# Three small moves in a two-layer attention kernel: row normalisation to GpSimd, an earlier pair of products, and masks written by ScalarE

## What is computed

```python
x = x + L0_xattn(layernorm(x), ctx, ctx)          # 16 heads, no mask
x = x + L0_ffn(layernorm(x))
x = x + L1_xattn(layernorm(x), ctx, ctx, mask)    # logits + mask * -1e9
x = x + L1_moe(layernorm(x))

def act_quant(x):                                 # in L0_ffn, for each row
    scale = 127.0 / clip(max(abs(x)), 1e-05)
    return clip(round(x * scale), -128, 127) / scale
```

## Time and profile before

| | |
|---|---|
| median of 3 runs | 509.7 us (509.5 to 510.54) |
| the profiled execution | 508.18 us |
| its span, first to last instruction | 506.4 us |
| PE busy | 443.3 us (88%) |
| PEld busy | 363.2 us (72%) |
| DVE busy | 345.9 us (68%) |
| ACT busy | 301.6 us (60%) |
| POOL busy | 226.5 us (45%) |
| mean granted clock of TensorE | 0.981 |

### The profile page before, as it was taken

One profiled execution on the slowest core, in us unless ns is written; L12 is line 12 of the kernel. 1 busy time (PEld: TensorE's weight loads), 2 busy tenths in 40 slices (PEclk: granted clock), 3 DMA queues, 4 the chain that ended last, 5 costly groups with the idle time before them and its releaser, 6 DMA issues.

```text
span 506.4 us, 11481 instructions
## 1 busy us (share of the span) xinstructions
PE 443.3 (88%) x3709; PEld 363.2 (72%) x3709; DVE 345.9 (68%) x1233; ACT 301.6 (60%) x649; POOL 226.5 (45%) x455
## 2 busy tenths in 40 slices
PE   3689999999998779967999999999999889899960
PEld 2477777777775668856778878777777579899960
DVE  6767787878783267877887788787878266444424
ACT  5237776767767448874466756566556555455630
POOL 4752464123216245767200225354453566666650
PEclk9999999999999989989999999999999999999995
DMA  6463323332405995034253234333320301332107
GB/s 216 150 223 105 115 85 116 102 101 77 137 4 207 426 415 213 2 105 130 84 159 113 88 107 158 118 122 94 112 61 2 87 23 39 85 85 82 53 15 249
DMA packets 40698, 61.55 MB, mean 122 GB/s; under 512 B 6121, under 2 KB 30506, under 8 KB 39232
## 3 DMA queue, kind: packets, MB, share of 16 engines
q1 hardware_dynamic: 38080, 56.20, 34.0%
q0 software_dynamic: 2272, 4.24, 2.6%
q10 hardware_dynamic: 288, 0.39, 0.3%
HBM read 31.45 MB, written 29.23 MB: 120 GB/s over the span
## 4 chain that ended last, share of the span: by engine, by line
PE 45%; DVE 10%; issue 5%; ACT 4%; DMA 3%; SPq 2%; POOL 1%; POOLq 0%; DVEq 0%; ACTq 0%
PE ps L1698 6%; PE ps L1658 6%; PE ps L1740 6%; PE ps L1743 5%; PE ps L1889 5%; PE ps L1900 5%; ACT probs L1023 2%; PE ps L1867 1%; DMA k_blocks<-y_dram 1%; DVE ps L1303 1%; PE ps L1954 1%; PE ps L1674 1%; SPq L544 1%; PE ps L1675 1%; PE ps L1676 1%
## 5 line engine op out<-in xcount | busy, mean ns | idle before, releaser
L1023 ACT ACTIVATE probs<-ps 128x512 f32<-128x512 f32 x256 | 147.0, 598 | 79.6 <-PE ps L1743 75.0
L1658 PE MATMUL ps<-k_blocks,q_stacks 128*128 128x256 f32 x512 | 117.9, 314 | 6.4 <-DVE row_max L1289 3.0
L1289 DVE TENSOR_REDUCE row_max<-ps 128x2 f32<-128x512 f32 x144 | 94.9, 686 | 26.9 <-PE ps L1658 25.7
L1743 PE MATMUL ps<-q_stacks,k_blocks 128*128 128x256 f32 x512 | 104.9, 288 | 1.2 <-DMA q_stacks<-maxT 1.0
L1303 DVE CUSTOM_DVE_ANT_0 ps<-ps,mask_q 128x256 f32<-128x256 f32 x224 | 89.8, 452 | 20.6 <-PE ps L1658 18.9
L1743 PEld LDWEIGHTS ps<-q_stacks,k_blocks 128*128 128x128 f32 x512 | 86.8, 189 | 20.8 <-issue 10.6
L1658 PEld LDWEIGHTS ps<-k_blocks,q_stacks 128*128 128x128 f32 x512 | 82.6, 197 | 13.9 <-issue 4.3
L1698 PE MATMUL ps<-probs,v_aug 128*32 128x256 f32 x1024 | 68.5, 385 | 4.3 <-ACT probs L1023 3.1
L817 POOL TENSOR_SCALAR max_split<-row_max 128x16 fp32r<-128x16 f32 x32 | 6.5, 204 | 124.3 <-issue 93.0
L1740 PE MATMUL ps<-mask_k,neg_mask_eye 128*128 128x512 f32 x128 | 54.5, 426 | 0.0
L739 POOL DMA_INDIRECT y_dram<-x_ring x39 | 39.1, 1003 | 22.6 <-ACT x_ring L1102 14.2
(11 more groups left out here) (217 smaller groups left out, 760.1 us busy)
## 6 DMA issues: line engine op xcount, KB each, us to landing
slots_dram<-x_ring SPq DMA_DIRECT2D x1, 10400.0 KB, 30.1
q_stacks<-q_dram SPq DMA_DIRECT2D x32, 256.0 KB
k_blocks<-k_dram SPq DMA_DIRECT2D x128, 48.0 KB
q_dram<-qk_parts SPq DMA_DIRECT2D x16, 256.0 KB, 2.9
k_dram<-qk_parts SPq DMA_DIRECT2D x16, 256.0 KB, 2.9
mask_in<-host_mask SPq DMA_DIRECT2D x8, 512.0 KB, 3.6
experts<-host_experts SPq DMA_DIRECT2D x1, 4096.0 KB, 39.1
x_ring<-slots_dram SPq DMA_DIRECT2D x39, 65.0 KB
```

What stands on the lines that cost most here:

```text
L1023: eng.activation(probs[:, n // HPS % 2, n % HPS, :, :].rearrange("p k q -> p (k q)"), ps[:, head_bank(BANKS_T, n)[0], :], ACT.Exp).then_in ...
L1289: eng.tensor_reduce(row_max[:, :, n], ps[:, head_bank(BANKS_S, n)[0], :].rearrange("p (i k) -> p i k", i=NT), AX.X, ALU.max).then_inc(a.s_ ...
L1658: mm = eng.matmul(ps[:, bank, i * S:(i + 1) * S], q_stack[r][:, st, i * P:(i + 1) * P], k_blocks[r][:, st, j, :], start=not masked, stop=n ...
L1743: mm = eng.matmul(ps[:, bank, k * S:(k + 1) * S], k_blocks[r][:, st, j, k * P:(k + 1) * P], q_stack[r][:, st, :], start=(l == 0), stop=(l ...
```

## The change

Three edits.

1. **Layer 0's `ln_apply`** goes from VectorE (n = 11) to GpSimd, right behind `ln_power`. `quant_factors` stays on VectorE at n = 13 and waits for it.
2. **Layer 0, step 1 of each body on TensorE**: `shifted` of head 1 and then the transposes of half 1's maxima stand ahead of `weighted_v`. Before, the transposes stood at step 0 and `shifted` of head 1 behind `weighted_v`. ScalarE's `out_copy` of half 1 moves from n = 0 to n = 1.
3. **Layer 1**: for the heads 5, 7, 8, 11, 13 and 15 the mask matmul is gone. ScalarE writes `-320000 * mask_k` into the bank (`mask_seed`) at steps 2, 4, 5, 8, 10 and 12, behind the exponential that frees it, and the two products add to what stands there.

```diff
-    "max1": (0, 2),
+    "max1": (None, 2),
-    "a_out1": (0, 0),
+    "a_out1": (1, 0),
-    "d_ln": (11, 12),
+    "d_ln": (None, 12),
...
+        SEEDED = (5, 7, 8, 11, 13, 15)
+        SEED_STEPS = (2, 4, 5, 8, 10, 12)
...
                 if exists(b - 1):
                     ln_power(eng, s, b - 1)
+                    if l == 0:
+                        ln_apply(eng, s, b - 1)
...
+                    if l == 1 and exists(b) and n in SEED_STEPS:
+                        mask_seed(b, SEEDED[SEED_STEPS.index(n)])
...
+            def mask_seed(b, n):
+
+                if n == SEEDED[0]:
+                    eng.wait_ge(a.k_k, b + 1)
+                eng.wait_ge(a.p_sb, b * 16 + n - 2 if n < H - 1 else b * 16 + 12)
+                eng.activation(ps[:, head_bank(BANKS_T, n)[0], :],
+                               mask_k[b % 3][:, :, :].bitcast(F32).rearrange("p i k -> p (i k)"),
+                               ACT.Copy, scale=-MASK_A).then_inc(a.t_seed, 1)
...
                     if exists(b + 1):
                         scores(eng, l, b + 1, 1 - r, n)
+                    ahead = l == 0 and n == at["pv"] % HPS and exists(b)
+                    if ahead:
+                        shifted(b, r, n)
+                        second_max(b)
                     if n % HPS == at["pv"] % HPS:
...
-                    if exists(b):
+                    if exists(b) and not ahead:
                         shifted(b, r, n)
...
-                if l == 1:
+                seeded = l == 1 and n in SEEDED
+                if seeded:
+                    eng.wait_ge(a.t_seed, b * len(SEEDED) + SEEDED.index(n) + 1)
+                elif l == 1:
                     eng.matmul(ps[:, bank, :], neg_mask_eye[:, :], mask_k[b % 3][:, :, :].rearrange("p i k -> p (i k)"),
                                start=True, stop=False)
```

More of the change, by code:

```diff
@@ L320, in __init__ @@
                     return
+                self.t_seed = s("t_seed")
                 self.k_in, self.k_q, self.k_k = s("mask_in"), s("mask_q"), s("mask_k")
@@ L1340, in body @@
                         residual_stats(eng, l, b - 1)
[L1341 to L1345, removed]
+                    if l == 1 and n == at["d_ln"] and exists(b - 1):
+                        ln_rows(eng, b - 1, 1 - r)
                     if l == 0 and n == at["d_quant"] and exists(b - 1):
@@ L1721, in body, with second_max @@
                             weighted_v(eng, l, b, r, (n - at["pv"]) // HPS)
-                    if exists(b):
+                    if exists(b) and not ahead:
                         shifted(b, r, n)
                     extras(b, r, n)
+            def second_max(b):
+                if after(b, 0):
+                    eng.wait_ge(a.o_sb, b * 2 - 1)
+                max_transposes(eng, l, b, 1)
             def shifted(b, r, n):
@@ L1743, in shifted @@
                     mm = eng.matmul(ps[:, bank, k * S:(k + 1) * S], k_blocks[r][:, st, j, k * P:(k + 1) * P],
-                                    q_stack[r][:, st, :], start=(l == 0), stop=(l == 0 or k == NT - 1))
+                                    q_stack[r][:, st, :], start=(l == 0), stop=(l == 0 or k == NT - 1),
+                                    skip_group_check=seeded)
                 mm.then_inc(a.t_ps, 1)
@@ L1762, in extras @@
                 if n == at["max1"] and exists(b):
-                    if after(b, 0):
-                        eng.wait_ge(a.o_sb, b * 2 - 1)
-                    max_transposes(eng, l, b, 1)
+                    second_max(b)
                 if n == at["qk"] and two_ahead(l, b):
```

## The result

The changed kernel took **507.74 us** in the median of 20 runs (505.31 to 511.17), the kernel before 509.72 in 20 runs between them (508.29 to 513.47): 0.9956 of its time, 95% interval 0.9939 to 0.9973, so 2.0 us faster by the medians (1.4 to 3.1 by the interval) where 4.9 were forecast. The direction is right and the time lies in the range; the size is off by more than half. They are not always the quotient of the two medians shown, and differences in us are worked out from the ratios where nothing else is said.

The account below looks back on a forecast made before the run. The prediction took TensorE to set the pace in both layers, with two waits in each layer 0 body. Its terms, +1.0 - 2.7 - 5.0 + 1.8 = -4.9 us, took 509.7 to 504.8 us, range 500.0 to 510.0.

Parts of the forecast that it names:

- Edit 1: Layer 0's normalised rows moved from VectorE to POOL: forecast +1.0 us in all.
- Steady bodies: Layer 0's steady bodies with rows on POOL: quantising factors start at the same time, a tie, 0 us.
- End of layer 0: Nothing covers the last two rows there: 1.60 us on POOL instead of 0.60 on VectorE, +1.0 us.
- The third rival, POOL late: Layer 0: rows on POOL take longer beside VectorE, delaying eight bodies; 517.6 us at twice the time; chance 0.06.
- Edit 2: Layer 0: head 1's products fill TensorE's hole before the transposes, 0.47 us in a steady body, -2.7 us together.
- Edit 3: Layer 1's six seeds: 0.71 us a body over seven bodies, -5.0 us, before the last body's cost.
- Heads 13 and 15: Layer 1: TensorE dense there with VectorE ahead, so both masks count, 2 x 0.24 = 0.47 us a body.
- The zeros for heads 5, 8 and 11: Layer 1: these masks lie inside or beside waits for other engines, so removing them gains 0.
- the 0.24 for head 7: Layer 1: this head's mask lies behind the wait for VectorE, so removing it gains 0.24 us a body.
- The rival in which VectorE binds all of layer 1: Layer 1: scores go at VectorE's pace with two banks, so seeds give nothing; 509.8 us; chance 0.11.
- Body 7: Layer 1's last body: seeds lengthen ScalarE's path, about 0.5 us plus 2 x 0.65 before the tanh, +1.8 us.
- The sum: Whole kernel: +1.0 - 2.7 - 5.0 + 1.8 = -4.9 us, forecast 504.8 us.

Follow-up runs that it names:

- the order alone: Kernel before with only head 1's two products and half 1's transposes moved in layer 0, rows on VectorE, no seeds: 508.16 us, ratio 0.9952.
- the two better kernels above: Kernel before with layer 0's new order, seeds for heads 7 and 13 except last body; rows on VectorE (0.9861), or on POOL for seven batches (0.9858).
- the seventh run: Changed kernel with one more 128x128 row on VectorE in each body of layer 1, behind head 12's maximum: 509.31 us in one run, bodies 20.41 us.

## Why the prediction came out as it did

**Edit 1, right.** Steady bodies 0 forecast, and 0 measured: 0.27 us less over layer 0's bodies, but that is a standstill of VectorE of 0.36 us, which goes from a body of layer 0 to one of layer 1 (last section). End of layer 0 +1.0 forecast, +1.06 measured (4.00 to 5.06). The third rival, POOL late, fell: a row took 806 ns beside VectorE's maxima. The rule of the Trainium skill behind it ("Perfetto Trace Analysis", Optimizing Scalar/DVE Operations) shows no effect in this trace.

**Edit 2, right.** -2.7 forecast. The transposes of body 1 and body 7 were 103.73 us apart and are 101.12, -2.6; by the projections -2.2, of which the order alone gives -2.0, and its own kernel is 2.5 us faster by the runs. A steady body gave 0.42 us and not 0.47. The transposes' wait went in the steady bodies, head 0's stayed.

**Edit 3, the step that failed.** "Heads 13 and 15: dense, with VectorE ahead. 2 x 0.24 = 0.47." One of the two counts. VectorE was ahead, idle for 0.55 us before head 14's maximum, and I took that for room. But it was idle because it waited for these very scores; the trip scores, maximum, scores through two banks took 1.60 us of TensorE's 1.65. The term should have been 2 x 0.24 = 0.48 a body, head 7 and head 13, and not 0.71: 7 x 0.48 = -3.4 in place of -5.0. The steady bodies show the 0.48. That the whole stretch to the seventh projection is 3.4 us shorter as well is in part luck. It also holds 0.5 for body 7's seeds and the 0.36 of VectorE's standstill, so the seeds brought some 4.3 us there; in the two better kernels above, which have neither, it is 3.8 and 3.9 us shorter. The surplus over 3.4 lies in the first and last bodies, where traces of one kernel also differ by up to 0.6 us. The zeros for heads 5, 8 and 11 and the 0.24 for head 7 stand in the steady bodies. Two masks give 0.48 (20.88 to 20.40), so a mask is worth 0.24, not the 0.13 of the Trainium skill's sustained spacing ("TensorE: Matmul & The Clock Gate", Back-to-back issue gap). The rival in which VectorE binds all of layer 1 named the right engine and the two banks, but let them eat all of the gain, by VectorE's amount of work, and that the seventh run excludes. (A small slip in the same part: from the first issue at 150.68 to the product at 153.05 it is 2.37 us, not 2.35. No `shifted` waited for a DMA in layer 1.)

**Body 7, right.** +1.8 forecast as 0.5 + 2 x 0.65; measured 0.5 + 1.2. What these seeds cost through the clock behind them, the prediction left out; by the traces it may be 1 us more.

**The sum.** With two masks in place of three the forecast would have been +1.0 - 2.7 - 3.4 + 1.8 = -3.3 us, where -4.9 stood. The four stretches measured give the same, -2.2 + 1.06 - 3.4 + 1.2 = -3.3 (body 7's 0.5 is in the -3.4). The runs gave -2.0 and -4.1 on two chips. The rest is the clock, which falls in some stretches outside the steady bodies, and in one execution of a kernel not in the same ones as in the next. In 56 runs of the kernel before on the chips of the experiments, the 24 with a mean clock of 0.973 to 0.977 took 510.0 us in the mean, the 7 at 0.967 or less 512.2. Of the changed kernel's 28, the 12 of the first class took 506.2, the 10 of the second 509.4: -3.8 and -2.8 at like clocks (in the second class 0.965 and 0.962 in the mean, so the changed kernel's were a little slower). That the change has no part in how often the clock falls isn't shown: two comparisons disagree on it (0.968 and 0.972), and the window behind body 7 speaks for a part.

## What to carry to other kernels

An engine that is idle before its step of a ping-pong isn't ahead: add up the whole round trip (product, reduction, next product in the same bank) and set it beside the other engine's work in between, since only that difference can be gained. Then offload the few instructions that count: two seeds of six gave the whole gain of a steady body, and the other four cost 0.5 us (heads 5, 8 and 11) and 0.6 us (head 15) in the last body, where nothing covered them. And leave the last pass of a loop as it was when an offload there has no partner to hide behind: the seeds of heads 13 and 15 cost 0.6 us each there, and the two rows on POOL 1.06 together, the whole difference between the two engines.

## What I had not expected of the hardware

- In one body of layer 1, always the same, VectorE stood still between two instructions with nothing to wait for, 0.25 us in this timeline of the changed kernel:

```profile
330.66 0.47 DVE L1279 RECIPROCAL rden<-ps 128x16 f32<-128x16 f32 x2 [0.52 <-PE ps L1877]
331.38 0.61 DVE L1285 TENSOR_TENSOR o_norm<-ps,rden 128x64 f32<-128x64 f32 x4 [0.25 <-issue]
```

  That body takes 0.36 us longer (20.75). It is so in all eight traces of kernels that take just layer 0's sixteen row instructions off VectorE, and in none of the other six: not with the rows left there, not with the last batch's two left there, and not with more VectorE work in layer 1. But the four with all sixteen left on VectorE lose the same 0.36 us in layer 0, between the third and the fourth projection (17.59 us in the kernel before, 17.22 to 17.24 in its neighbours). In the kernel before, the statistics of one batch and of the next:

```profile
78.36 0.49 DVE L428 BATCH_NORM_STATS2 ln_st<-x_res 128x6 f32<-128x128 f32 x2
...
95.95 0.49 DVE L428 BATCH_NORM_STATS2 ln_st<-x_res 128x6 f32<-128x128 f32 x2 [0.50 <-DVE x_res L1282]
```

  VectorE waits there only for its own instruction just ahead, 0.50 us where it is 0.14 in the other bodies. So the standstill isn't new with the change, it moved. It goes with the place of the instruction in VectorE's program; what happens at that place no run shows.
- Executions of one kernel differ by over 1% in time, the kernel before from 507.4 to 513.1 us in the experiments, and go by how often the clock fell; single comparisons of 20 and 8 runs gave 0.9956 and 0.9920. Distances between marks in the steady bodies repeat to some 0.1 us, and told apart what the runs couldn't.
